# Batches of six decay factors in a ring of twelve tiles, with a new slot table, in a one-core decoder layer

## The reference

```python
def step(h, inps):
    x_t, d_t, B_t, C_t = inps
    bar_A = jnp.exp(jnp.minimum(d_t[:, :, None] * A, 2.0))
    bar_B = jnp.clip(d_t[:, :, None] * B_t[:, None, :], -2.0, 2.0)
    h = jnp.clip(bar_A * h + bar_B * x_t[:, :, None], -100.0, 100.0)
    y = jnp.sum(h * C_t[:, None, :], axis=-1) + x_t * D_param
    return (h, y)
...
routing = jax.nn.softmax(flat @ Wr + br, axis=1)
hid = jax.nn.silu(jnp.einsum('nd,edf->enf', flat, up_w) + up_b[:, None, :])
all_out = jnp.einsum('enf,efd->end', hid, down_w) + down_b[:, None, :]
```

## Time and profile before

| | |
|---|---|
| median of 3 runs | 455.79 us (453.95 to 459.5) |
| the profiled execution | 454.75 us |
| its span, first to last instruction | 453.0 us |
| mean granted clock of TensorE | 0.886 |
| TensorE busy | 340.5 us (75%) |
| VectorE busy | 300.1 us (66%) |
| ScalarE busy | 254.3 us (56%) |
| GpSimd busy | 218.8 us (48%) |

### The profile page before, as it was taken

One profiled execution on the slowest core, in us unless ns is written; L12 is line 12 of the kernel. 1 busy time (PEld: TensorE's weight loads), 2 busy tenths in 40 slices (PEclk: granted clock), 3 DMA queues, 4 the chain that ended last, 5 costly groups with the idle time before them and its releaser, 6 DMA issues.

```text
span 453.0 us, 5945 instructions
## 1 busy us (share of the span) xinstructions
PE 340.5 (75%) x1749; PEld 229.6 (51%) x1749; DVE 300.1 (66%) x908; ACT 254.3 (56%) x438; POOL 218.8 (48%) x237
## 2 busy tenths in 40 slices
PE   1447657598986998995989999870537999999560
PEld 1213333264654655653656767660327856868360
DVE  4689998968999799999387386468238202222156
ACT  1857336977779798786465575620205575554012
POOL 4435755475356455426336032724673636465523
PEclk9999956989998899998689999896557999999866
DMA  4879800000000000000000000110112322210153
...
DMA packets 29474, 23.96 MB, mean 53 GB/s; under 512 B 5448, under 2 KB 23943, under 8 KB 29440
## 3 DMA queue, kind: packets, MB, share of 16 engines
...
## 4 chain that ended last, share of the span: by engine, by line
PE 53%; DVE 17%; ACT 13%; issue 7%; POOL 4%; DMA 3%; DVEq 1%; SPq 0%; POOLq 0%; ACTq 0%
PE bank L1515 10%; PE bank L1506 9%; PE bank L1749 6%; PE bank L1737 6%; PE bank L1497 4%; ACT a L1280 3%; DVE bank L575 3%; POOL slots_in L1157 2%; DVE acc L679 2%; PE bank L1708 2%; PE bank L1596 2%; PE bank L1697 1%; ACT hid L1301 1%; DVE hc L623 1%; DVE stats L434 1%
## 5 line engine op out<-in xcount | busy, mean ns | idle before, releaser
L1169 POOL TENSOR_TENSOR yD<-yD,hc 128x512 f32<-128x512 f32 x64 | 83.1, 1298 | 82.7 <-DVE hc L623 76.1
L1506 PE MATMUL bank<-yD,w 128*128 128x512 f32 x128 | 71.2, 640 | 10.3 <-ACT hid L1301 10.3
L588 DVE TENSOR_TENSOR_SCAN h<-a,bank 128x512 f32<-128x512 f32 x64 | 77.8, 1215 | 1.5 <-ACT a L1280 1.1
L1515 PE MATMUL bank<-w,hid 128*128 128x128 f32 x512 | 72.4, 287 | 1.0 <-DVE acc L679 1.0
L1515 PEld LDWEIGHTS bank<-w,hid 128*128 128x128 f32 x512 | 66.0, 199 | 12.3 <-issue 9.0
L1497 PE MATMUL bank<-rows,selid 99*128 99x512 bf16 x128 | 51.4, 464 | 16.8 <-DVE hc L623 8.5
L1301 ACT ACTIVATE hid<-bank,cols 128x512 f32<-128x512 f32 x64 | 43.1, 684 | 26.0 <-PE bank L1506 15.8
L575 DVE TENSOR_TENSOR bank<-bank,u 128x512 f32<-128x512 f32 x64 | 43.6, 681 | 19.4 <-PE bank L1497 19.4
...
L1127 POOL TENSOR_TENSOR rstd<-vpe,nhalf 128x4 f32<-128x4 f32 (+1 forms) x19 | 20.9, 1098 | 56.7 <-DVE nmr L444 43.8
L1497 PEld LDWEIGHTS bank<-rows,selid 99*128 99x128 bf16 x128 | 14.0, 110 | 61.6 <-DVE hc L623 22.8
L623 DVE TENSOR_TENSOR hc<-h,bank 128x512 f32<-128x512 f32 x64 | 43.3, 677 | 1.4 <-PE bank L1497 1.4
...
## 6 DMA issues: line engine op xcount, KB each, us to landing
...
```

The lines of the kernel that those rows point to most:

```text
L588: ins = v.tensor_tensor_scan(state_of(k), decay_of(k).rearrange("p j n -> p (j n)"), drive_of(k), 0.0, ALU.mult, ALU.add)
L1169: pool.tensor_tensor(grp(yD, g), grp(yD, g), read_of(k), ALU.add).then_inc(summed, 1)
L1506: pe.matmul(bank[UP_BANKS[f % 2]][:, 0:width(g)], w1[:, e, f * P:(f + 1) * P], grp(yD, g), start=True, stop=True).then_inc(up_ps, 1)
L1515: ins = pe.matmul(bank[DOWN_BANK][:, j * P:(j + 1) * P], hid[:, m % 2, f, j * P:(j + 1) * P], w2[:, e, f, :], start=(f == 0), stop=(f == F ...
```

## The change

The ring has twelve tiles, eight in `a` and four more over `xe_early` and `xe_tok`, two buffers that hold token rows of the second mixture and are empty during the scan. The first column of the four is set to zero like that of the others, by two more memsets among the constants. Batches have six units (the last four), so there are eleven in place of sixteen. The tables PRE, MIX, KV and ATT and the list DECAYS have new numbers at some places.

```diff
-A_RING, A_BATCH, HC_RING, H_RING = 8, 4, 3, 3
+A_RING, A_BATCH, HC_RING, H_RING = 12, 6, 3, 3
...
-    {"DVE": {5: 6, 11: 10, 12: 12, 14: 14, 0: 0},
+    {"DVE": {5: 6, 11: 11, 12: 12, 14: 15, 0: 0},
...
-    {"DVE": {0: 38, 2: 40, 3: 41, 4: 42, 9: 47, 13: 53, 14: 54, 17: 57, 19: 60, 22: 62},
-     "POOL": {0: 38, 3: 41, 5: 43, 13: 51, 14: 54},
-     "ACT": {1: 39, 4: 42, 5: 44, 6: 45, 10: 49, 11: 51, 14: 54, 15: 55, 18: 57},
-     "PE": {5: 44, 6: 45, 7: 46, 11: 51, 12: 52, 15: 55, 16: 56, 20: 57}},
+    {"DVE": {0: 38, 2: 40, 3: 41, 4: 42, 9: 48, 13: 53, 14: 53, 17: 56, 19: 59, 22: 61},
+     "POOL": {0: 38, 3: 41, 5: 43, 13: 51, 14: 53},
+     "ACT": {1: 39, 4: 42, 5: 44, 6: 45, 10: 50, 11: 52, 14: 53, 15: 54, 18: 56},
+     "PE": {5: 43, 6: 45, 7: 46, 11: 51, 12: 52, 15: 54, 16: 55, 20: 56}},
...
-DECAYS = [-4, 0, 2, 6, 12, 15, 20, 24, 27, 31, 36, 40, 44, 49, 53, 56]
+DECAYS = [-4, 2, 6, 12, 18, 25, 31, 37, 47, 49, 55]
...
-        a = sb("a", [P, A_RING, GT, P])
+        a = sb("a", [P, A_RING - 4, GT, P])
...
+        a_more = [t[:, 0:2 * GW].rearrange("p (k j n) -> p k j n", k=2, j=GT)
+                  for t in (xe_early[:].rearrange("p e n -> p (e n)"), xe_tok[:].rearrange("p b j n -> p (b j n)"))]
...
-    N_CONST = 13
+    N_CONST = 15
...
         def decay_of(k):
-            return a[:, k % A_RING, 0:SIZES[k // NS], :]
+            r = k % A_RING - (A_RING - 4)
+            t = a[:, k % A_RING] if r < 0 else a_more[r // 2][:, r % 2]
+            return t[:, 0:SIZES[k // NS], :]
...
             const(pool.memset(a[:, :, :, 0:1], 0.0))
+            for t in a_more:
+                const(pool.memset(t[:, :, :, 0:1], 0.0))
...
-                for j in (j for j in range(UNITS // A_BATCH) if DECAYS[j] == k):
-                    for i in range(A_BATCH * j, A_BATCH * (j + 1)):
+                for j in (j for j in range(len(DECAYS)) if DECAYS[j] == k):
+                    for i in range(A_BATCH * j, min(UNITS, A_BATCH * (j + 1))):
                         decay(i)
```

32 lines of the change are left out of this document (16 added, 16 removed).

## The result

The changed kernel took **467.88 us** (465.98 to 470.51, 4 runs) beside 455.88 us (453.95 to 459.5, 4 runs) for the kernel before: ratio 1.026, 95% interval 1.020 to 1.032. Measured again beside another set of runs it took 467.06 us (462.14 to 470.27) against 455.51, ratio 1.021 (1.016 to 1.026). The first median lies 0.4 us above the range, the second inside.

The account below looks back on a forecast made before the run. VectorE and its waits were taken to bound up to slot 57, then TensorE, then a chain through all engines. Seven terms summed to +5.7 us on 454.75, giving 460.5 us; own range 457 to 464, wider range 448.0 to 467.5.

Parts of the forecast that it names:

- term 2: Slots 11 to 24: added loads, decays and a B/C projection wait hidden by existing waits; 0 us, bounds -1.8 and +1.
- term 4: Slots 35 to 41: more loads and Exp work delay the activation that TensorE awaits; +1.0 us, bounds -0.7 and +2.
- term 7: Tail behind the scan: placing of group 2 moves to cover a wait for the root; -0.9 us, bounds -2 and 0.
- term 6: Slots 54 to 57: TensorE's accumulation starts later (+4.3), other work gets shorter (-3.7); +0.6 us, bounds -6.9 and +4.3.
- The loads: ScalarE's table loads: 44 before and after, none saved; batches mostly lose neighbouring Exp work, so load only moves.
- Term 1: Start: two more memsets on GpSimd before the constants are released; +0.2 us, bounds 0 and 0.3.
- Term 3: Slot 31: decide stands straight before its flag is read, 1.1 us partly hidden; +0.6 us, bounds 0 and 1.1.
- Term 5: Slots 46 to 53: ScalarE's batches delay the softmax copy and VectorE's attention add; +4.2 us, bounds 0 and +7.
- slower: TensorE's clock: Rival: TensorE drops to the lower clock after waits over about 2 us in slots 48 to 53; 465.5 us, chance 0.20.
- 468: Upper figure of the clock rival: the same clock loss once more before slot 57.
- 445: Rival, chance 0.18: the drive's wait at 222.45 dissolves, 448.8 us; 445 if term 2 gives 1.8 and term 4 nothing.
- sign: Expected evidence: 44 loads, idle before scans 16 and 32, scan 48 waiting, late attention add, slot 57's drive waiting over 6 us.

Follow-up runs that it names:

- after: Profile of the changed kernel itself, one execution; the kernel's median is 467.88 us, ratio 1.026 to the kernel before.
- w81_warm: The changed kernel with the last eight matmuls of slot 81, ahead of the transposes behind the scan, issued twice: 463.79 us, ratio 1.017.
- b1_slots_kv43: The kernel before with the new slot tables, but group 1's context transposes kept in slot 43; old ring and batches: 457.77 us, ratio 1.002.
- d1_batch53: The changed kernel with one batch, units 54 to 59, moved from slot 49 to slot 53: 463.92 us, ratio 1.015.
- b3_flag_early: New slot tables, old ring and batches, context transposes in slot 43, and decide one slot earlier (slots 14 and 30): 457.29 us, ratio 1.000.
- s1_slots_only: The kernel before with all new slot tables, but the old ring of eight and batches of four: 460.99 us, ratio 1.012.
- s3: The changed kernel with four batches moved by 1 to 4 slots to stand beside other Exp work: 463.35 us, ratio 1.017.
- w38: The changed kernel with eight matmuls of slot 38 issued four times in place of once: 467.77 us, ratio 1.028.

## Why the prediction was wrong

In after the span grew by 14.9 us where the sum had 5.7. The 9.2 us between them lie in term 2 (3.2 us over the forecast), term 4 (2.2) and term 7 (4.6), less 0.6 in term 6 and small amounts elsewhere. In the execution of w81_warm, 2.4 us over the sum, they lie in terms 2 and 4 (1.5 each) and 7 (0.6), less 0.6 in term 6 and 0.7 in slots 58 to 63. So the sign was right, and three terms were too small, each for a step that failed.

- **The loads** (44 before and after, none saved) and that the batches lose their neighbours of the same table set: right. With the old slots the batches alone lose as much as the whole change, but 4.4 us of it in slot 9, which the new slots mend; the new slots alone lose 1.2%, and 0.2% with the context transposes put back (b1_slots_kv43). The two do not add up place by place.
- **Term 1**, +0.2: +0.08 at scan 0.
- **Term 2**, 0 forecast, +0.9 to +3.9 measured up to scan 30 in the four profiles of this program. Failed step: "a wait of some 1.5 us inside the same cover" (the cover being waits that VectorE has there anyway). At a clock of 1.00 ahead of the projection the wait had the size forecast (1.30 and 1.48) and most of it was covered, with +0.9 and +1.6 left; but I had not asked what the cover hangs on. The batch at slot 18 makes TensorE wait 1.65 us two activations earlier than the one I looked at. In after and d1_batch53 the clock then stays down for most of the next 15 us (0.61 and 0.63 from 82 to 97, 0.77 and 0.82 in the other two), the projection comes 2.8 us late, the next drives wait for slower row broadcasts as well, and it is +3.3 or +3.9. In w81_warm the same wait, 1.79 us, was followed by the full clock; why is open. The clock stood among my rivals, but for slots 48 to 53.
- **Term 3**, +0.6: +0.8 in every profile of this program (scan 30 to 32), 1.21 us idle at scan 16 and 0.84 at scan 32. Right; b3_flag_early takes both away.
- **Term 4**, +1.0 forecast, +3.2 measured (2.5 in w81_warm's execution). The first link was right: the activation was forecast at 151.1, with the 3.5 us of delay at scan 38 that makes 154.6, and it ended at 153.79 + 0.69 = 154.5; the drive that waits for it lost 1.2 us against before. The failed step is that I stopped there. Behind the activation on ScalarE stand a normalisation, a product and the copy of the row that frees TensorE's bank, and all came late too; the next drive waited 1.25 us and the expert's add 1.49. s1_slots_only, with the same slots and no batch at 37, loses nothing there.
- **Term 5**, +4.2: measured +4.16, with the add 4.1 us later as worked out, scan 48 waiting 1.93 us. Here the whole queue had been counted along, and that was not luck: the activation of slot 46 ended at 187.35 where I had 180.5, 6.9 us later with the delay carried in, and the copy at the end of the queue at 209.99 where I had 202.9, 7.1 us later.
- **Term 6**, +0.6: measured 0.0, and the drive of slot 57 waits 6.00 us, at the edge of what I had said ("over 6"). Whether its two halves, +4.3 and -3.7, were right was not taken apart. b1_slots_kv43 and s1_slots_only show that the new slots save 1.5 us here when the old batches stay.
- **Term 7**, -0.9 forecast, +3.7 in after, -0.3 in w81_warm. The move itself gave what was forecast: from the last expert's add to the centring 10.13 us in place of 11.09. Two things were missed. Of the placed rows' writes on GpSimd two were issued ahead of the centring before and none now, so all of them stand ahead of the next root, which comes 1.08 us later against its statistics and takes the gain back. And the lower clock behind the wait of 1.71 us costs 3.2 us: from scan 63 to the last add it takes 63.2 to 63.4 us in the six profiles that have it there, and 60.14 or 60.15 in the three with the new slots and the same wait that do not (s3, w38, d1). In w81_warm, where the clock stays up, the end gains 0.3 us in all. The failed step of term 7 is that it priced the moved work alone: it left out the writes that the next root then stands behind, and put TensorE's clock behind the scan at nothing.
- **The rivals.** The time was that of "slower: TensorE's clock" (465.5 to 468), but by luck as to the place: the clock cost time in slots 19 to 24 and behind the scan, which I had not named, and some in slots 37 to 42, while in slots 47 to 53, where I put it, it stayed at 1.00 in after. The point that I gave, a wait of about 2 us, was not borne out: in after the lower clock followed waits of 1.65 and 1.71 us and the full one waits of 1.79 and 1.81. Two sums there were off: 445 should be 446, and 468, "the same once more" on 465.5, would be 470.5 at the same price. Nearly every sign that I had listed came true, and still the sum was too low: they all lay at the places that I had costed.
- **The base.** The sum was made on a profiled execution of 454.75 us, from the lower group of before's times. The changed kernel's executions reach from 462.1 to 470.5 us, which goes with the clock in slots 19 to 25 and behind the scan; the profile of w81_warm, with 462.84 us, is 8.1 us above that base, the one of after, with 469.63, 14.9. My 5.7 was a sum for the shorter kind, and its own range, to 464, had no room for the longer.
